# Turning x on VectorE in 32x32 squares through memory, and ScalarE's own SiLU for convolution and gate

## The chip, the cores and the metric

The kernel runs on one core of a Trainium2 chip. A core has TensorE (PE, matrix products, preceded by weight loads, PEld), VectorE (DVE), ScalarE (ACT), GpSimd (POOL) and SyncE (SP), which here only issues DMAs. Every engine works through its own list of instructions in order, and they meet only at semaphores. The metric is the device time of one execution in microseconds. The kernel before takes 1625.1 us, the median of three runs (1624.51 to 1627.74).

## The reference

The input is four sequences of 256 tokens with 512 channels. A small feed-forward layer (a base matrix and two of eight LoRA experts, picked for each token) stands before and after a Mamba2 mixer. Nearly all the time is in the mixer, cut here to what matters:

```python
proj = hidden_states @ in_proj_w.T                     # 512 -> 8192 (gate) + 10240 (x, B, C) + 128 (dt)
gate, xBC, dt = jnp.split(proj, [INTER, INTER + CONV_DIM], axis=-1)
conv = jax.lax.conv_general_dilated(xBC_t, conv_w, window_strides=(1,), padding=[(K - 1, 0)],
                                    feature_group_count=CONV_DIM)        # 4 taps, each channel by itself
xBC = jax.nn.silu(jnp.swapaxes(conv + conv_b[None, :, None], 1, 2))
x, Bm, Cm = jnp.split(xBC, [INTER, INTER + NG * SS], axis=-1)
# in chunks of 128 tokens, 128 heads of 64 channels in 8 groups:
Lmat = jnp.where(tri, jnp.exp(seg), 0.0)               # decay between two tokens
scores = jnp.einsum('bclhn,bcshn->bchls', Cc, Bc) * Lmat
Ydiag = jnp.einsum('bchls,bcshp->bclhp', scores, xdt)  # xdt = x * dt
y = Ydiag + Yoff + x * D
yg = y * jax.nn.silu(gate)
rstd = jax.lax.rsqrt(jnp.mean(jnp.square(yg_g), axis=-1, keepdims=True) + EPS)   # over a group of 1024
out = ((yg_g * rstd).reshape(Bsz, S, INTER) * norm_w) @ out_proj_w.T
```

silu(v) is v * sigmoid(v). Everything is float32.

## The kernel before

The projections are done in three passes of a rounded format (high times high, high times low, low times high), so each block of 128 input channels is three matmuls of 512 columns (L159 to L161). The two chunks of a sequence are treated as one block of 256 tokens with a causal mask, so no state is carried.

The mixer goes over 8 groups (index g) of 1024 channels and 16 heads. A group starts with four units (B and C, each for two halves of the tokens), which need the same projection, convolution and SiLU; then come 16 steps (index st). A step is one tile of 128 channels (two heads) for one half of the tokens, 512 columns. In a step, TensorE does the projection of x for the step four ahead (unit st+5, `project`), the projection of the gate (`project_gate`), the output projection of one tile of 128 tokens (`project_out`, in the first group only from step 8 on), and `mix_tokens`, which multiplies the 256x256 matrix of decays and scores with x. `mix_tokens` wants x with tokens on the partitions, whereas projection and convolution leave it with channels there. So a step begins with `transpose_x` (L1441): four 128x128 matmuls with the identity.

The other engines in a step, each in the order of its own list:

- ScalarE: four exponentials of 256 columns, the decay for the next step (`decay_from_first`, L1108, waits for the mask and for the `mix_tokens` that last used the slot); rounding of a weight tile (L834); in the steps from 9 on a copy of a finished output half (L1148); evacuation of the projection of x, times the last tap (L877); square of the gated y of the step before (L1140); rounding of a y tile for the output projection (L1131); four exponentials of 128 columns (`decay_from_second`, L1118); tanh for the gate (L1125); tanh for the convolution (L1097); in even steps the rounding of an output weight (L1088).
- VectorE: y plus D times x (`skip_y`, L1280), the product of decays and scores (`make_mix`, L1262), x times dt out of PSUM (`scale_x`, L1269), three taps of the convolution (L892), the rest of the SiLU for the gate (L1286) and for the convolution (L1244), in odd steps an output weight (L1290), in steps 1 to 8 two additions of the group before (L1309, L1316).
- GpSimd: the causal mask on the first diagonal (`mask_diagonals`, L1021, needs only its DMA) and on the second (L1025, waits for `mix_tokens`), both for the next step; y times gate (`gate_y`, L1033); the low part of a weight (L839); the low part of a y tile (`split_tile`, L1038); the running sum of squares (`sum_squares`, L1046, from step 3 on).
- SyncE: a weight tile (256 KB), the decay rows (512 KB, waits for L1118) and in odd steps an output weight (256 KB).

The group ends with a tail: the rest of the projections of the next group's B, C and first x, and the mean square, for which ScalarE loads the table of Sqrt (`root`, L1152) and then that of Exp again.

SiLU is computed as v/2 * (1 + tanh(v/2)); the halves are put into the taps, D and dt beforehand (`conv_constants`, `head_constants`). Tanh and Exp are in one table, so the steps load none.

Of the kernel before, what the change touches and what calls it, by code (L numbers as in the profile page):

```python
# [790 lines left out]
class InProj:  # L791
# [3 lines left out]
    def __init__(self, nc, ctx, m, w_in, conv_w, conv_b, d_skip):  # L795
        def sb(name, shape, dt=F32):
# [103 lines left out]
def mixer_phase(nc, m, ip, norm_w, w_out, ncs_dram, next_ln):  # L900

    with ExitStack() as ctx:
# [65 lines left out]
        def _(sp):  # L968
# [110 lines left out]
        def _(act):  # L1079
            start_at_one(act, [s["th"], s["tg"], s["decay"], s["sq"], s["wohi"], s["gcopy"], s["root"]])  # L1080
# [527 lines left out]
```

## Time and profile before

| | |
|---|---|
| median of 3 runs | 1625.1 us |
| profiled execution, its span | 1627.01 us, 1625.2 us |
| PE busy | 1564.3 us, 96% |
| PE weight loads busy | 1226.0 us, 75% |
| DVE busy | 1228.0 us, 76% |
| POOL busy | 1052.0 us, 65% |
| ACT busy | 1002.3 us, 62% |
| mean granted TensorE clock | 0.989 |
| DMA | 131.65 MB, mean 81 GB/s |

The span is what the trace covers; 1.8 us of the execution lie around it. Matmuls are pipelined: a matmul of 512 columns has a record of some 0.39 us, but the next one starts 0.23 us after it, so the sum of a group's records is more than the time it holds the engine. ScalarE's and VectorE's records overlap a little too, by about 0.1 us, and what an instruction costs in a row of others is the distance between two starts.

### The profile page before, as it was taken

The numbers are of one execution on the slowest core, as the hardware profiler recorded it, in microseconds if no ns is written. First come the engines' busy times: TensorE is split into PE (matmuls) and PEld (weight loads), VectorE is DVE, ScalarE is ACT, GpSimd is POOL, SyncE is SP. The second block draws the span as 40 slices with busy tenths as digits, with TensorE's granted clock in tenths as the row PEclk, the third lists the DMA queues.
The fourth block names the chain that finished last, engine by engine and source line by source line (L and its number), as shares of the span: only waits on it lengthen the run. The fifth ranks groups of instructions, "written<-read, shape, count | busy, mean of one in ns | idle before, by whom it ended". The sixth has DMA issues, their size and how long they took to land. (4 is left out here: it accounts for less than half of the span.)

```text
span 1625.2 us, 25474 instructions
## 1 busy us (share of the span) xinstructions
PE 1564.3 (96%) x8296; PEld 1226.0 (75%) x8296; DVE 1228.0 (76%) x1689; ACT 1002.3 (62%) x2122; POOL 1052.0 (65%) x790
## 2 busy tenths in 40 slices
PE   6979999999999999999999999999999999999979
PEld 4657777777777777777777777777777777777757
DVE  6688877787778877887688877887688877887565
ACT  4357765666666665666666665666666665666431
POOL 2017874788757874788657874787657874787620
PEclk9899999999999999999999999999999999999989
DMA  3033321323222221222212321223222221322011
GB/s 118 1 103 103 107 91 59 92 91 92 78 72 92 92 92 59 91 92 92 78 72 92 92 91 59 92 92 92 78 75 88 92 92 59 98 86 84 20 40 53
DMA packets 73658, 131.65 MB, mean 81 GB/s; under 512 B 10944, under 2 KB 10944, under 8 KB 73280
## 3 DMA queue, kind: packets, MB, share of 16 engines
q1 hardware_dynamic: 73536, 130.09, 24.3%
q8 instruction: 68, 1.11, 0.3%
q14 instruction: 54, 0.44, 0.1%
HBM read 127.44 MB, written 2.62 MB: 80 GB/s over the span
## 5 line engine op out<-in xcount | busy, mean ns | idle before, releaser
L892 DVE SCALAR_TENSOR_TENSOR mx_acc<-bank,mx_cw,mx_acc 128x510 f32<-128x510 f32 (+2 forms) x480 | 358.3, 746 | 160.8 <-ACT mx_acc L877 149.5
L159 PE MATMUL bank<-h_hi,mx_w_hi 128*128 128x512 f32 x1152 | 465.6, 404 | 4.4 <-DVE mx_acc L892 2.3
L161 PE MATMUL bank<-h_hi,mx_w_lo 128*128 128x512 f32 x1152 | 453.1, 393 | 0.0
L160 PE MATMUL bank<-h_lo,mx_w_hi 128*128 128x512 f32 x1152 | 450.2, 391 | 0.0
L1108 ACT ACTIVATE mx_mix<-mx_csb,mx_gncs 128x256 f32<-128x256 f32 x512 | 218.9, 499 | 284.3 <-PE bank L1478 281.3
L1033 POOL TENSOR_TENSOR mx_y<-mx_y,mx_sg 128x512 f32<-128x512 f32 x128 | 338.4, 2644 | 59.7 <-DVE mx_y L1280 51.7
L839 POOL TENSOR_TENSOR mx_w_lo<-mx_w_raw,mx_w_hi 128x512 fp32r<-128x512 f32 x144 | 187.4, 1302 | 111.0 <-ACT mx_w_hi L834 111.0
L161 PEld LDWEIGHTS bank<-h_hi,mx_w_lo 128*128 128x128 f32 x1152 | 216.9, 188 | 48.5
L159 PEld LDWEIGHTS bank<-h_hi,mx_w_hi 128*128 128x128 f32 x1152 | 217.3, 189 | 47.8 <-issue 6.5
L160 PEld LDWEIGHTS bank<-h_lo,mx_w_hi 128*128 128x128 f32 x1152 | 217.7, 189 | 41.5
L1262 DVE TENSOR_TENSOR mx_mix<-mx_mix,mx_cbt 128x1536 f32<-128x1536 f32 x128 | 224.5, 1754 | 0.0
L1025 POOL TENSOR_SCALAR_AFFINE_SELECT mx_mix<-mx_csb 128x512 f32<-128x512 f32 x128 | 89.9, 702 | 202.0 <-PE bank L1478 202.0
L877 ACT ACTIVATE mx_acc<-bank,mx_cb,mx_cw 128x512 f32<-128x512 f32 x160 | 124.2, 777 | 140.9 <-PE bank L161 140.9
L159 PE MATMUL bank<-mx_wo_hi,mx_yt_hi 128*128 128x512 f32 x512 | 203.4, 397 | 7.3 <-POOL mx_yt_lo L1038 7.3
L1038 POOL TENSOR_TENSOR mx_yt_lo<-mx_y,mx_yt_hi 128x512 fp32r<-128x512 f32 x128 | 167.3, 1307 | 58.2 <-ACT mx_yt_hi L1131 58.0
L161 PE MATMUL bank<-mx_wo_hi,mx_yt_lo 128*128 128x512 f32 x512 | 202.0, 394 | 0.0
L160 PE MATMUL bank<-mx_wo_lo,mx_yt_hi 128*128 128x512 f32 x512 | 200.5, 392 | 0.0
L1021 POOL TENSOR_SCALAR_AFFINE_SELECT mx_csb<-mx_csb 128x512 f32<-128x512 f32 x128 | 123.2, 963 | 68.1 <-DMA mx_csb<-cs_rows 68.1
L1280 DVE SCALAR_TENSOR_TENSOR mx_y<-mx_acc,mx_dh,bank 128x512 f32<-128x512 f32 x128 | 95.3, 745 | 88.9 <-PE bank L1478 88.8
L1118 ACT ACTIVATE mx_mix<-mx_mix,mx_gncs 128x128 f32<-128x128 f32 x512 | 162.1, 389 | 0.0
L1474 PE MATMUL bank<-mx_mix,mx_xd 128*64 128x256 f32 x1024 | 160.5, 392 | 0.0
L1046 POOL TENSOR_TENSOR mx_ssum<-mx_ssum,mx_sq 128x512 f32<-128x512 f32 x112 | 148.2, 1323 | 1.1 <-ACT mx_sq L1140 1.1
(163 smaller groups left out, 2203.7 us busy)
## 6 DMA issues: line engine op xcount, KB each, us to landing
mx_csb<-cs_rows SPq DMA_DIRECT2D x128, 512.0 KB, 4.0
mx_w_raw<-in_w_in SPq DMA_DIRECT2D x144, 256.0 KB, 4.0
mx_wo_raw<-in_w_out SPq DMA_DIRECT2D x64, 256.0 KB, 4.2
res<-in_x SPq DMA_DIRECT2D x8, 256.0 KB, 5.0
f_base_raw<-in_base_wt SPq DMA_DIRECT2D x2, 1024.0 KB, 6.1
out<-res SPq DMA_DIRECT2D x8, 256.0 KB, 2.0
f_a_raw<-in_lora_a SPq DMA_DIRECT2D x2, 256.0 KB, 3.8
f_lb_raw<-in_lora_b SPq DMA_DIRECT2D x2, 256.0 KB, 6.2
```

The lines of the kernel that those rows point to most:

```text
L159: nc.tensor.matmul(out, w_hi, x_hi, start=first, stop=False)
L160: nc.tensor.matmul(out, w_hi, x_lo, start=False, stop=False)
L161: return nc.tensor.matmul(out, w_lo, x_hi, start=False, stop=last)
L839: self.nc.gpsimd.tensor_tensor(self.w_lo[:, w % 3, :, :], self.w_raw[:, w % 3, :, :], self.w_hi[:, w % 3, :, :].bitcast(F32), ALU.subtract ...
L892: self.nc.vector.scalar_tensor_tensor(dst, src[:, :, 0:SEQ - k], self.cw[:, c, TAPS - 1 - k:TAPS - k], dst, ALU.mult, ALU.add).then_inc(s[ ...
L1033: nc.gpsimd.tensor_tensor(y[:, st, :], y[:, st, :], sg[:, st % 2, :], ALU.mult).then_inc(s["yg"], 1)
L1038: nc.gpsimd.tensor_tensor(yt_lo[:, p % 2, :, :], y_tile(q, hf, t), yt_hi[:, p % 2, :, :].bitcast(F32), ALU.subtract).then_inc(s["ylo"], 1)
L1046: nc.gpsimd.tensor_tensor(ssum[:, i, :], ssum[:, i, :], sq[:, i, :], ALU.add).then_inc(s["ssum"], 1)
L1108: nc.scalar.activation(mix[:, i, hd, b, 0:SEQ], csb[:, i, hd, b * SEQ:(b + 1) * SEQ], ACT.Exp, bias=gncs[:, tile, head:head + 1], scale=-1.0)
L1118: last = nc.scalar.activation(mix[:, i, hd, b, SEQ:PAIR], mix[:, i, hd, b, SEQ:PAIR], ACT.Exp, bias=gncs[:, tile, head:head + 1], scale=-1.0)
L1262: nc.vector.tensor_tensor(a, a, both, ALU.mult).then_inc(s["mix"], 1)
L1474: nc.tensor.matmul(Y_BANK[i][rows, c0:c0 + SEQ], xd[:, i, 2 * b, hd, :], mix[:, i, hd, b, 0:SEQ], start=True, stop=False)
```

## The change

**x is no longer transposed on TensorE.** VectorE transposes each 32x32 square of the tile in place (`turn_squares`), writing x with the squares laid out by partition block. SyncE writes that tile, 256 KB, to a buffer in memory and reads it back with four DMAs, one for each block of 32 partitions, so that the squares come to lie in their transposed places (`move_x`). `scale_x` reads the result from SBUF instead of PSUM and stands behind the taps now, not in front of them.

**SiLU is one instruction on ScalarE** (`silu_conv`, `silu_gate`), in place for the convolution. The two VectorE instructions that finished it are gone, and so are the factors 0.5.

**ScalarE's list has another order.** The rounding of the y tile and the square of the step before stand at the end of the step, behind the SiLUs; before, they stood ahead of the second exponentials. The squares are written into the gate's buffer, which is free by then. The exponentials take their bias straight from the whole table `ncs`.

```diff
+            def move_x(g, st):
+                i, u = st % 2, st + 4
+                sp.wait_ge(s["turned"], 1 + STEPS * g + st + 1)
+                if not (first(g) and st < 2):
+                    x_moved(sp, *((g, st - 2) if st >= 2 else (g - 1, st + STEPS - 2)))
+                sp.dma_start(x_dram[i, :, :], xs[:, u % 2, :]).then_inc(x_out[i], 16)
+                step_slot_freed(sp, s["xd"], g, st)
+                sp.wait_ge(x_out[i], 16 * (XT * g + st // 2 + 1))
+                for q in range(P // SQ):
+                    src = x_dram[i, :, q * P:(q + 1) * P].rearrange("(i r) e -> r i e", r=SQ)
+                    sp.dma_start(xt[q * SQ:(q + 1) * SQ, i, :, :, :].rearrange("r i t c -> r i (t c)"),
+                                 src).then_inc(x_in[i], 16)
...
-            def tanh_conv(g, u):
+            def silu_conv(g, u):
                 act.wait_ge(s["tap"], 1 + (TAPS - 1) * (UNITS * g + u + 1))
-                act.wait_ge(s["conv"], 1 + UNITS * g + max(u - 1, 0))
-                nc.scalar.activation(th[:, u % 2, :], acc[:, u % 4, :, :].rearrange("p b t -> p (b t)"),
-                                     ACT.Tanh).then_inc(s["th"], 1)
+                a = acc[:, u % 4, :, :].rearrange("p b t -> p (b t)")
+                nc.scalar.activation(a, a, ACT.Silu).then_inc(s["conv"], 1)
...
-                nc.scalar.activation(sg[:, st % 2, :], G_BANK[:, :], ACT.Tanh, scale=0.5).then_inc(s["tg"], 1)
+                nc.scalar.activation(sg[:, st % 2, :], G_BANK[:, :], ACT.Silu).then_inc(s["sg"], 1)
...
+                    if here or more:
+                        decay_from_second(gn, stn)
+                    silu_gate(g, st)
+                    if here or more:
+                        silu_conv(gn, un)
+                    if st % 2 == 0:
+                        split_wo(g, st // 2)
+                    if here and has_tile(g, st + 1):
+                        round_tile(g, st + 1)
                     if st >= 1:
                         square(g, st - 1)
...
-                    if here and has_tile(g, st + 1):
-                        round_tile(g, st + 1)
...
+            def turn_squares(g, st):
+
+                u = st + 4
+                dve.wait_ge(s["conv"], 1 + UNITS * g + u + 1)
+                if not (first(g) and st < 2):
+                    x_moved(dve, *((g, st - 2) if st >= 2 else (g - 1, st + STEPS - 2)))
+                nc.vector.transpose(xs[:, u % 2, :].rearrange("p (q t c) -> p t q c", t=2 * HB, c=SQ),
+                                    acc[:, u % 4, :, :].rearrange("p b t -> p (b t)")).then_inc(s["turned"], 1)
...
                     make_mix(g, st)
-                    scale_x(g, st)
...
                         ip.taps(dve, gn, un)
-                    silu_gate(g, st)
-                    if here or more:
-                        silu_conv(gn, un)
+                    scale_x(g, st)
+                    if here:
+                        turn_squares(g, st + 1)
...
-                    transpose_x(g, st)
```

**ScalarE's list, a step from 9 on, before.** From the evacuation of the projection to the first exponentials of the next step. `mx_th` is the tanh of the convolution, `mx_sg` the gate, `mx_sq` the square, `mx_yt_hi` the rounded y tile; the brackets name the semaphores that an instruction waits for.

```order
L877 ACTIVATE mx_acc<-bank,mx_cb,mx_cw 128x512 [waits mx_ysb,mx_proj]
L1140 ACTIVATE mx_sq<-mx_y 128x512 [waits mx_ssum,mx_yg]
L1131 ACTIVATE mx_yt_hi<-mx_y 128x512 [waits mx_out,mx_yg]
L1118 ACTIVATE mx_mix<-mx_mix,mx_gncs 128x128 [waits mx_masked1]
L1118 ACTIVATE mx_mix<-mx_mix,mx_gncs 128x128 x3
L1125 ACTIVATE mx_sg<-bank 128x512 [waits mx_yg,mx_gate]
L1097 ACTIVATE mx_th<-mx_acc 128x512 [waits mx_conv,mx_tap]
L1108 ACTIVATE mx_mix<-mx_csb,mx_gncs 128x256 [waits mx_y,mx_masked0]
```

The same stretch now. L1143 and L1111 are the SiLUs of gate and convolution, L1149 rounds the y tile, L1156 is the square.

```order
L879 ACTIVATE mx_acc<-bank,mx_cb,mx_cw 128x512 [waits mx_ysb,mx_proj]
L1131 ACTIVATE mx_mix<-mx_mix,ncs 128x128 [waits mx_masked1]
L1131 ACTIVATE mx_mix<-mx_mix,ncs 128x128 x3
L1143 ACT_TABLE_LOAD [waits mx_ssum]
L1143 ACTIVATE mx_sg<-bank 128x512 [waits mx_gate]
L1111 ACTIVATE mx_acc<-mx_acc 128x512 [waits mx_tap]
L1149 ACTIVATE mx_yt_hi<-mx_y 128x512 [waits mx_out,mx_yg]
L1156 ACTIVATE mx_sg<-mx_y 128x512 [waits mx_yg]
L1121 ACT_TABLE_LOAD [waits mx_y]
L1121 ACTIVATE mx_mix<-mx_csb,ncs 128x256 [waits mx_masked0]
```

Two table loads stand in every step now, one before the SiLUs and one before the exponentials; the whole program had 22 and has 273. Square and y tile have moved from the middle to the end.

**GpSimd's list** keeps its order (only the buffer of the squares has another name). This is it now, around the border of two steps; it reads what ScalarE's moved instructions leave.

```order
L1052 TENSOR_TENSOR mx_yt_lo<-mx_y,mx_yt_hi 128x512 [waits mx_yhi]
L1060 TENSOR_TENSOR mx_ssum<-mx_ssum,mx_sg 128x512 [waits mx_ssum,mx_sq]
L1035 AFFINE_SELECT mx_csb<-mx_csb 128x4x128 [waits mx_cs_in1]
L1039 AFFINE_SELECT mx_mix<-mx_csb 128x4x128 [waits mx_y]
L1047 TENSOR_TENSOR mx_y<-mx_y,mx_sg 128x512 [waits mx_sg,mx_ysb]
```

L1035 is the first mask, for which ScalarE's L1121 waits (`mx_masked0`); it stands behind the sum of squares, as before.

**VectorE's list, an odd step from 9 on, before**, from `make_mix` to the next `make_mix`:

```order
L1262 TENSOR_TENSOR mx_mix<-mx_mix,mx_cbt 128x1536 [waits mx_decay]
L1269 TENSOR_TENSOR mx_xd<-bank,mx_gdt 128x512 [waits mx_y,mx_xt]
L892 SCALAR_TENSOR_TENSOR mx_acc<-bank,mx_cw,mx_acc 128x2x255 [waits mx_evac]
L892 SCALAR_TENSOR_TENSOR mx_acc<-bank,mx_cw,mx_acc 128x2x254 [waits mx_tap]
L892 SCALAR_TENSOR_TENSOR mx_acc<-bank,mx_cw,mx_acc 128x2x253 [waits mx_tap]
L1286 SCALAR_TENSOR_TENSOR mx_sg<-mx_sg,bank 128x512 [waits mx_tg]
L1244 SCALAR_TENSOR_TENSOR mx_acc<-mx_th,mx_acc 128x512 [waits mx_th]
L1290 SCALAR_TENSOR_TENSOR mx_wo_lo<-mx_wo_raw,mx_nw,mx_wo_hi 128x512 [waits mx_wohi]
L1280 SCALAR_TENSOR_TENSOR mx_y<-mx_acc,mx_dh,bank 128x512 [waits mx_ylo,mx_y]
L1262 TENSOR_TENSOR mx_mix<-mx_mix,mx_cbt 128x1536 [waits mx_decay]
```

and now:

```order
L1272 TENSOR_TENSOR mx_mix<-mx_mix,mx_cbt 128x1536 [waits mx_decay]
L894 SCALAR_TENSOR_TENSOR mx_acc<-bank,mx_cw,mx_acc 128x2x255 [waits mx_evac]
L894 SCALAR_TENSOR_TENSOR mx_acc<-bank,mx_cw,mx_acc 128x2x254 [waits mx_tap]
L894 SCALAR_TENSOR_TENSOR mx_acc<-bank,mx_cw,mx_acc 128x2x253 [waits mx_tap]
L1288 TENSOR_TENSOR mx_xd<-mx_xt,mx_gdt 128x4x4x32 [waits mx_y,mx_x_in1]
L1280 STREAM_TRANSPOSE mx_xs<-mx_acc 128x4x4x32 [waits mx_x_in0,mx_conv]
L1304 SCALAR_TENSOR_TENSOR mx_wo_lo<-mx_wo_raw,mx_nw,mx_wo_hi 128x512 [waits mx_wohi]
L1299 SCALAR_TENSOR_TENSOR mx_y<-mx_acc,mx_dh,bank 128x512 [waits mx_ylo,mx_y]
L1272 TENSOR_TENSOR mx_mix<-mx_mix,mx_cbt 128x1536 [waits mx_decay]
```

The scaling of x (L1288) stands behind the taps, and the turning of the next x (L1280) behind it, waiting for ScalarE's SiLU.

## Rows read from the trace of the kernel before

**Rows 1.** Windows: two steps of group 0, one whole group (each column: busy us, instructions).

```profile
145.95:162.28 16.33, 15.18 (x88) 11.63 (x88) 13.96 (x18) 12.13 (x27) 13.39 (x10) 1.00 0.35 113
465.06:647.25 182.19, 180.39 (x978) 142.29 (x977) 141.39 (x180) 117.94 (x253) 129.74 (x96) 1.00 0.26 85
```

**Rows 2.** Timeline of PE at a step's border (start, duration, line).

```profile
715.64 0.66 PE L1447 MATMUL bank<-ident,mx_acc 128*128 128x128 f32 x4
716.06 0.48 PE L159 MATMUL bank<-h_hi,mx_w_hi 128*128 128x512 f32 x1
```

**Rows 3.** Timeline of ACT, a whole even step from 9 on (brackets: idle before, releaser).

```profile
564.50 1.71 ACT L1108 ACTIVATE mx_mix<-mx_csb,mx_gncs 128x256 f32<-128x256 f32 x4 [3.01 <-PE bank L1478]
566.11 0.62 ACT L834 ACTIVATE mx_w_hi<-mx_w_raw 128x512 fp32r<-128x512 f32 x1
566.64 0.58 ACT L1148 ACTIVATE gacc<-bank 128x512 f32<-128x512 f32 x1
567.79 0.78 ACT L877 ACTIVATE mx_acc<-bank,mx_cb,mx_cw 128x512 f32<-128x512 f32 x1 [0.58 <-PE bank L161]
568.47 0.62 ACT L1140 ACTIVATE mx_sq<-mx_y 128x512 f32<-128x512 f32 x1
568.99 0.62 ACT L1131 ACTIVATE mx_yt_hi<-mx_y 128x512 fp32r<-128x512 f32 x1
569.51 1.26 ACT L1118 ACTIVATE mx_mix<-mx_mix,mx_gncs 128x128 f32<-128x128 f32 x4
570.68 0.58 ACT L1125 ACTIVATE mx_sg<-bank 128x512 f32<-128x512 f32 x1
571.16 0.62 ACT L1097 ACTIVATE mx_th<-mx_acc 128x512 f32<-128x512 f32 x1
571.68 0.71 ACT L1088 ACTIVATE mx_wo_hi<-mx_wo_raw,mx_nw 128x512 fp32r<-128x512 f32 x1
574.79 1.71 ACT L1108 ACTIVATE mx_mix<-mx_csb,mx_gncs 128x256 f32<-128x256 f32 x4 [2.39 <-PE bank L1478]
```

**Rows 4.** Timeline of ACT around a table load in a tail.

```profile
279.41 0.63 ACT L1097 ACTIVATE mx_th<-mx_acc 128x512 f32<-128x512 f32 x1 [2.00 <-DVE mx_acc L892]
280.06 1.28 ACT L1152 ACT_TABLE_LOAD   x1
281.35 0.21 ACT L1152 ACTIVATE mx_rms<-mx_rms 128x8 f32<-128x8 f32 x1
```

**Rows 5.** Timeline of POOL in the step of rows 3.

```profile
569.69 1.30 POOL L1038 TENSOR_TENSOR mx_yt_lo<-mx_y,mx_yt_hi 128x512 fp32r<-128x512 f32 x1 [0.42 <-ACT mx_yt_hi L1131]
570.95 1.30 POOL L1046 TENSOR_TENSOR mx_ssum<-mx_ssum,mx_sq 128x512 f32<-128x512 f32 x1
572.20 1.09 POOL L1021 TENSOR_SCALAR_AFFINE_SELECT mx_csb<-mx_csb 128x512 f32<-128x512 f32 x1
575.56 2.74 POOL L1033 TENSOR_TENSOR mx_y<-mx_y,mx_sg 128x512 f32<-128x512 f32 x1
```

**Rows 6.** Timeline of DVE in the same stretch.

```profile
571.90 0.90 DVE L1244 SCALAR_TENSOR_TENSOR mx_acc<-mx_th,mx_acc 128x512 f32<-128x512 f32 x1
575.39 1.75 DVE L1262 TENSOR_TENSOR mx_mix<-mx_mix,mx_cbt 128x1536 f32<-128x1536 f32 x1
578.89 2.31 DVE L892 SCALAR_TENSOR_TENSOR mx_acc<-bank,mx_cw,mx_acc 128x510 f32<-128x510 f32 x3 [1.15 <-ACT mx_acc L877]
```

**Rows 7.** Single lines: duration in ns, least/median/most, of all their instructions.

```profile
L1021 POOL TENSOR_SCALAR_AFFINE_SELECT mx_csb<-mx_csb x128: 624/1087/1105, 102.5 to 1514.0; 128x512 f32<-128x512 f32 x128
L1033 POOL TENSOR_TENSOR mx_y<-mx_y,mx_sg x128: 1261/2734/2792, 122.6 to 1535.2; 128x512 f32<-128x512 f32 x128
L1244 DVE SCALAR_TENSOR_TENSOR mx_acc<-mx_th,mx_acc x160: 679/891/1605, 101.0 to 1524.0; 128x512 f32<-128x512 f32 x160
L1316 DVE SCALAR_TENSOR_TENSOR res<-gacc,mx_rms,res x64: 744/752/1760, 299.2 to 1575.7; 128x512 f32<-128x512 f32 x64
```

**Rows 8.** DMA issues: KB each, median us from issue to landing.

```profile
mx_csb<-cs_rows SPq DMA_DIRECT2D x128, 512.0 KB, 4.0
```

More of the change, by code:

```diff
@@ L53 @@
 PAIR = SEQ + CH
+SQ = 32
+CONSTS = 7
 NE, RANK = 8, 16
@@ L800, in __init__ @@
         self.s = semaphores(nc, ctx, "mx", [
-            "const_in", "nw_in", "const", "proj", "gate", "xt", "y", "cb", "out", "ss",
-            "evac", "th", "tg", "decay", "sq", "yhi", "whi", "wohi", "gcopy", "root",
+            "const_in", "nw_in", "const", "proj", "gate", "turned", "y", "cb", "out", "ss",
+            "evac", "decay", "sq", "yhi", "whi", "wohi", "gcopy", "root",
             "tap", "conv", "mix", "xd", "sg", "ysb", "cbt", "gsum", "outsb", "ms", "inv", "wolo",
@@ L907, in mixer_phase @@
         wo_in = [ctx.enter_context(nc.semaphore(f"mx_wo_in{i}")) for i in range(2)]
+        x_out, x_in = ([ctx.enter_context(nc.semaphore(f"mx_x_{n}{i}")) for i in range(2)] for n in ("out", "in"))
         cs_in = [ctx.enter_context(nc.semaphore(f"mx_cs_in{i}")) for i in range(2)]
@@ L1005, in group @@
                         ip.load_constants(sp, g + 1)
+                    move_x(g, st)
                 if more:
                     load_late(g + 1)
-            loop_groups(sp, group)
+            for g in range(NG):
+                group(g, g + 1 < NG)
         @block.gpsimd
@@ L1079, in _ @@
         def _(act):
[L1080 removed]
+            start_at_one(act, [s["conv"], s["sg"], s["decay"], s["sq"], s["wohi"], s["gcopy"], s["root"]])
             start_after_quad(act, [s["yhi"]])
@@ L1116, in decay_from_second, with silu_gate @@
                     for hd in range(2):
-                        tile, head = 2 * (HB * hf + b) + 1, 2 * j + hd
+                        tile, head = 2 * (HB * hf + b) + 1, GH * g + 2 * j + hd
                         last = nc.scalar.activation(mix[:, i, hd, b, SEQ:PAIR], mix[:, i, hd, b, SEQ:PAIR], ACT.Exp,
-                                                    bias=gncs[:, tile, head:head + 1], scale=-1.0)
+                                                    bias=m.ncs[:, tile, head:head + 1], scale=-1.0)
                 last.then_inc(s["decay"], 1)
-            def tanh_gate(g, st):
+            def silu_gate(g, st):
                 act.wait_ge(s["gate"], 1 + STEPS * g + st + 1)
-                act.wait_ge(s["yg"], 1 + STEPS * g + max(st - 1, 0))
-                nc.scalar.activation(sg[:, st % 2, :], G_BANK[:, :], ACT.Tanh, scale=0.5).then_inc(s["tg"], 1)
+                if st >= 4:
+                    act.wait_ge(s["ssum"], 1 + SUMS * g + st - 3)
+                elif st >= 2:
+                    act.wait_ge(s["yg"], 1 + STEPS * g + st - 1)
+                elif not first(g):
+                    act.wait_ge(s["ssum"], 1 + SUMS * g - 1 + st)
+                nc.scalar.activation(sg[:, st % 2, :], G_BANK[:, :], ACT.Silu).then_inc(s["sg"], 1)
             def round_tile(g, p):
@@ L1232, in _ @@
         def _(dve):
-            start_at_one(dve, [s["conv"], s["mix"], s["xd"], s["sg"], s["ysb"], s["cbt"],
+            start_at_one(dve, [s["turned"], s["mix"], s["xd"], s["ysb"], s["cbt"],
                                s["ms"], s["inv"], s["wolo"]])
@@ L1422, in _ @@
         def _(pe):
-            start_at_one(pe, [s["gate"], s["xt"], s["y"], s["cb"], s["ss"]])
+            start_at_one(pe, [s["gate"], s["y"], s["cb"], s["ss"]])
             start_after_quad(pe, [s["out"]])
@@ L1439, in b_dot_c @@
                 last.then_inc(s["cb"], 1)
-            def transpose_x(g, st):
-                pe.wait_ge(s["conv"], 1 + UNITS * g + st + 5)
-                if st == 0:
-                    pe.wait_ge(s["ms"], 1 + g)
-                pe.wait_ge(s["xd"], 1 + STEPS * g + st)
-                for t in range(2 * HB):
-                    last = nc.tensor.transpose(T_BANK[:, t * P:(t + 1) * P],
-                                               acc[:, st % 4, t // 2, t % 2 * CH:(t % 2 + 1) * CH], m.ident[:, :])
-                last.then_inc(s["xt"], 1)
             def project_gate(g, st):
@@ L1555, in program @@
 def program(nc, x, w_in, w_dt, conv_w, conv_b, dt_bias, d_skip, norm_w, w_out, base_wt, router_wt, lora_a, lora_b,
-            ncs_dram, out):
+            ncs_dram, x_dram, out):
     m = Chip()
```

120 lines of the change are left out of this document (46 added, 74 removed).

## The prediction

> **What bounds the kernel now.** I read the windows first. A whole group takes 182.19 us and TensorE is busy in 180.39 of them at full granted clock, the other engines in 118 to 141 [rows 1]. TensorE sets the time, so 7 groups at 182.19 and a shorter first one make up nearly all of the span. The step is next, in ScalarE's timeline: from one first L1108 to the next 10.29 us pass (564.50 to 574.79), and before each it sits idle for 3.01 or 2.39 us until the matmuls of L1478 end [rows 3]. ScalarE is ready 2.4 to 3 us early. In group 0, steps without an output projection take 16.33 / 2 = 8.17 us [rows 1]. The third view is GpSimd in the same step: its mask for the next step, L1021, ends at 572.20 + 1.09 = 573.29, 1.5 us before the L1108 that needs it [rows 5, 3]. These two margins are what the change spends.
>
> **Part 1, the transposes go.** From the first transpose to the first projection 0.42 us pass (715.64 to 716.06) [rows 2]. TensorE's step shrinks from 10.29 to about 9.85 us, -0.42 x 128 = -54 us if nothing else comes to bound.
>
> **Part 2, two table loads a step.** A step's ScalarE work before, from the distances of starts [rows 3]: 1.61 (L1108), 0.53 (L834), 0.48 (L1148, 0.58 less the 0.1 that neighbours overlap), 0.68 (L877), 0.52 (L1140), 0.52 (L1131), 1.17 (L1118), 0.48 (L1125), 0.52 (L1097), 0.61 (L1088): 7.1 us, 6.5 in odd steps, 0.48 less in steps up to 8. A load takes 1.28 us, starts 0.02 us after the end of the instruction before (279.41 + 0.63 = 280.04 to 280.06), and the next starts 0.01 us after it [rows 4]; it also undoes one overlap of 0.1. So 1.41 us each. For the SiLU instructions I take tanh's durations; half to twice of them would be -0.5 to +1.1 us a step. ScalarE then has 8.8 to 9.9 us of work in a step, on average 9.4: by itself it would just fit under TensorE's 9.85.
>
> The Trainium skill, "ScalarE: Activation LUTs", section "What ACT_TABLE_LOAD costs", adds a drain of 1380 ns to the load's 1283 ns. The 0.02 us ahead of the load in rows 4 don't show it; with it the forecast below would be 1.38 x 124 = 171 us longer.
>
> **Part 3, the new order closes a loop through GpSimd.** L1021 for step st+2 stands on GpSimd behind the sum of squares of st-1, and that behind the low part of the y tile st+1. Both now wait for the last instructions of ScalarE's step, and the next step's exponentials wait for L1021. So a step from 3 on can't be shorter than: ScalarE from its exponentials to the end of the y tile, then GpSimd's three instructions. With t = 0 at the first exponential (odd step up to 8, no L1148, no L1088): L834 at 1.61, L877 at 2.13, second exponentials 2.81 to 4.08, load 4.10 to 5.38, gate 5.39, convolution 5.87 (its taps began at 2.95 and are done at 5.3, 2.31 us [rows 6]), y tile 6.39 to 7.01. GpSimd starts 0.08 us after the y tile's end (568.99 + 0.62 = 569.61 to 569.69) [rows 3, 5]: 7.09. Then 1.26 and 1.25 us, the distances of its starts, and 0.62 for L1021, its least [rows 5, 7]: 10.22, plus 0.07 to ScalarE's start: 10.29. Even steps have L1088 as well (+0.6), steps from 9 on L1148 (+0.48): 10.29, 10.89, 10.77, 11.37. The second load hides in this wait: the square ends at 7.5, the load at 8.8.
>
> **Part 4, what VectorE does meanwhile.** `gate_y` takes 1.26 us at least but 2.73 in the median [rows 7]: L1033 began at 575.56, 0.17 us into L1262, which ended at 577.14, and itself ended at 578.30, 1.16 us later [rows 5, 6]. It stood still for the whole of L1262. The other way round L1244, 0.68 alone, took 0.90 when it began at 571.90 during the sum of squares (to 572.25), and L1021 behind it 1.09 for 0.62 [rows 5 to 7]. All these VectorE instructions read two operands in SBUF. So one works while the other waits, in the order of asking.
>
> The Trainium skill, "SBUF — State Buffer", section "SBUF: two separate sides", calls this an exclusive lock between GpSimd and VectorE instructions with two SBUF inputs, held to the instruction's end. Rows 5 and 6 agree; by a shared bandwidth the sum would be that of the next rival.
>
> Before, L1262 met only `gate_y`, which nobody waited for. Now the three GpSimd instructions end the step, where VectorE has its output weight (odd, 0.75), the addition L1316 (steps 1 to 8, 0.75 [rows 7]) and L1262 (1.75). I take the turning as an instruction of one operand that holds nobody up, of 0.69 us like one of 512 columns; its bounds are 0.5 and twice that. In turn, in us from t = 0:
> - odd, to 8: y tile to 8.4; output weight asked 7.2, runs to 9.1; squares to 10.35; L1316 asked 9.8, runs to 11.07; mask to 11.6. Step 11.7.
> - even, to 8: y tile 7.7 to 9.0; L1316 to 9.7; squares to 10.95; L1262, asked at 10.35, to 12.65; mask to 13.2. Step 13.25.
> - odd, from 9: y tile to 8.9; output weight to 9.6; squares to 10.85; L1262 to 12.55; mask to 13.1. Step 13.15.
> - even, from 9: y tile 8.2 to 9.5; L1262 to 11.2; squares to 12.4; mask to 13.05. Step 13.1.
>
> **Part 5, the way through memory.** A turned tile leaves VectorE at t = 7.2 to 7.7 and is wanted by `scale_x` behind the taps, at 5.3 of the next step: 10 to 11 us of room. No row shows such a transfer. The nearest is the 512 KB load with 4.0 us from issue to landing [rows 8]; a write and a read at that make 8, and three more issues at some 0.4 us each 9.2 us as upper end, perhaps 4 at the lower. I take 7, hidden in the steps. At a group's start nothing covers it: `scale_x` of step 0 follows the last turn directly, and I charge 2 us a group (0 to 4). `scale_x` and `mix_tokens` end at about t = 8, before the mask, so neither the moved scaling nor TensorE's wait for it is late. SyncE waits for the write before it can issue the next decay rows; these are wanted a step later than they land. Four small copies of constants at a group's border are below 1 us.
>
> **The sum.** Steps 3 to 14 of a group: 3 x (11.7 + 13.25) + 3 x (13.15 + 13.1) = 153.6 against 12 x 10.29 = 123.5: +30.1. Steps 1 and 2 have no sum of squares in the chain and gain together 0.4. The start costs 2. In the last step TensorE ends at t = 7.8 and not at 10.3, and the tail follows it: -2.5. Together +29.2, x 7 = +204. Group 0: steps 7 and 8 +4.4, 9 to 14 +17, steps 3 to 6 (no y tile: 9.65 and 11.25, against 8.17) +9.1, start and steps 0 to 2 +6: +36.5. In all 1625.2 + 241 = 1866 us of span, 1868 of execution. The profiled execution is 1.9 us above the median, which I take off: **1866 us**.
>
> **The rivals.**
> - *The lock costs less.* If VectorE's operands delay the chain not at all, the steps are 10.29 to 11.37, on average 10.83, +5.4 a group after start and tail, group 0 +16: 1625 + 38 + 16 = 1679. Half of the lock gives about 1770. For it: the order of asking in part 4 is worked out, and an instruction that comes 0.3 us earlier slips in ahead. Against it: rows 5 and 6. 20% for the stretch between 1680 and 1790.
> - *Faster.* If the mask doesn't hang on the moved instructions as I read it, because GpSimd gets square and y tile early enough (it would need to get them 2 us earlier than in part 3), then TensorE's 9.85 us bound and ScalarE's 9.4 fit: 1625 - 54 + 16 (eight starts through memory) = 1587. It decides where the chain of part 3 falls under 9.85. For it: all engines have less than 9.9 us of work. Against: the chain without any lock is 10.29 at least. 8% for everything under 1622.
> - *The change does nothing measurable*, gain and loop in balance: 2%.
> - *Memory or the clock bounds.* If the way through memory takes over 11 us, each us more costs 1 us x 120 steps; or a load costs more than in rows 4; or TensorE, now idle for a quarter of a step, is granted less. 10% for more than 1900, some 1960.
>
> 60% are left for 1790 to 1900 with 1866 as its value. Range over all: 1700 to 1905. What a measurement of this kernel can tell is about 0.2%, 3 us: faster 0.08, same 0.02, slower 0.90.
>
> **What will show it.** In ScalarE's timeline the time before the first exponentials of a step is ended by GpSimd's mask, no longer by L1478's matmuls, some 2 to 4 us of it; the load before them costs nothing extra and lies in that wait, the load before the gate follows at once on the second exponentials. The step is 11.7 to 13.3 us long. L1021's counterpart has a median of 0.6 to 2.3 us. TensorE's waits in the steps are ended by the scaling of x, 2 to 3 us a step, and its busy share falls to 80 to 85%. 256 table loads of 1.28 us are in the steps' code. I am wrong if the exponentials wait for TensorE, if ScalarE has no idle time in a step, or if `scale_x` waits for its DMA in the middle of a group.

## The result: 1863.4 us, 14.6% slower, and the profile after

| | before | after |
|---|---|---|
| median of 4 runs each, us | 1626.07 (1624.51 to 1627.74) | 1863.36 (1862.45 to 1865.07) |
| ratio after to before, 95% interval | | 1.146 (1.144 to 1.148) |
| profiled execution: time and span, us | 1627.01, 1625.2 | 1862.45, 1860.6 |
| a whole group, us | 182.19 [rows 1] | 210.97 |

The head of the page of the changed kernel (busy us, share of the span, instructions):

```profile
span 1860.6 us, 24204 instructions
PE 1581.7 (85%) x7784; PEld 1215.5 (65%) x7784; DVE 1226.8 (66%) x1545; ACT 1321.1 (71%) x2373; POOL 1047.1 (56%) x790
```

A window over its first whole group, from one L1168 table load in a tail to the next. The columns, as in [rows 1]: start and end, length, then busy us (instructions) of PE, PEld, DVE, ACT and POOL, granted clock of TensorE, busy share of the DMA engines, GB/s.

```profile
316.99:527.96 210.97, 186.63 (x915) 143.65 (x913) 141.05 (x161) 157.38 (x285) 129.34 (x97) 0.94 0.35 113
```

TensorE was busy in 99% of a group and is now busy in 88%, with 63 fewer instructions. Its granted clock over the group is 0.94, where it was 1.00 [rows 1]. No engine is full: as the rows below show, the step is a ring of engines that wait for each other. Its waits (engine, line, what ended the wait: total us, times, longest):

```profile
POOL mx_yt_lo L1052 <- ACT mx_yt_hi L1149: 430.8, 118, 7.5
DVE mx_acc L894 <- ACT mx_acc L879: 421.2, 152, 6.5
ACT mx_mix L1121 <- POOL mx_csb L1035: 262.3, 106, 3.4
PE bank L1466 <- DVE mx_xd L1288: 235.4, 101, 6.5
```

Third row: ScalarE's first exponentials wait for GpSimd's mask 106 times. In [rows 3] TensorE ended that wait. One step (even, below 9), first ScalarE (compare [rows 3]), then GpSimd [rows 5], then VectorE [rows 6]. Here and below `...` stands for rows left out, and a row of exponentials with x2 or x1 in place of x4 is cut off by the end of the view:

```profile
572.63 1.71 ACT L1121 ACTIVATE mx_mix<-mx_csb,ncs 128x256 f32<-128x256 f32 x4 [1.86 <-POOL mx_csb L1035]
...
575.43 1.27 ACT L1131 ACTIVATE mx_mix<-mx_mix,ncs 128x128 f32<-128x128 f32 x4
576.71 1.28 ACT L1143 ACT_TABLE_LOAD   x1
578.01 0.60 ACT L1143 ACTIVATE mx_sg<-bank 128x512 f32<-128x512 f32 x1
578.50 0.62 ACT L1111 ACTIVATE mx_acc<-mx_acc 128x512 f32<-128x512 f32 x1
...
579.63 0.62 ACT L1149 ACTIVATE mx_yt_hi<-mx_y 128x512 fp32r<-128x512 f32 x1
580.15 0.62 ACT L1156 ACTIVATE mx_sg<-mx_y 128x512 f32<-128x512 f32 x1
580.79 1.28 ACT L1121 ACT_TABLE_LOAD   x1
585.48 0.91 ACT L1121 ACTIVATE mx_mix<-mx_csb,ncs 128x256 f32<-128x256 f32 x2 [3.40 <-POOL mx_csb L1035]
```

```profile
580.33 1.31 POOL L1052 TENSOR_TENSOR mx_yt_lo<-mx_y,mx_yt_hi 128x512 fp32r<-128x512 f32 x1 [3.12 <-ACT mx_yt_hi L1149]
581.59 1.74 POOL L1060 TENSOR_TENSOR mx_ssum<-mx_ssum,mx_sg 128x512 f32<-128x512 f32 x1
583.29 2.16 POOL L1035 TENSOR_SCALAR_AFFINE_SELECT mx_csb<-mx_csb 128x512 f32<-128x512 f32 x1
```

```profile
580.55 1.64 DVE L1330 SCALAR_TENSOR_TENSOR res<-gacc,mx_rms,res 128x512 f32<-128x512 f32 x1
...
582.77 2.18 DVE L1272 TENSOR_TENSOR mx_mix<-mx_mix,mx_cbt 128x1536 f32<-128x1536 f32 x1
```

Follow the ring: exponentials 572.63, load, gate, convolution, y tile to 580.25; GpSimd's low half from 580.33; the sum; the mask, which asks at 583.29 while VectorE's L1272 runs to 584.95, and ends at 585.45; exponentials at 585.48. The step is 12.85 us. In the same rows VectorE and GpSimd take turns, and the one that begins while the other runs lasts longer: L1330 (0.75 alone) ends 0.55 us after L1052, L1060 1.14 us after L1330, L1272 1.62 us after L1060, L1035 0.50 us after L1272.

### The profile page after: what moved, and what is told of

Its sections match the earlier page's. It is cut to its first block and busy times, and to the rows that moved or that the text cites. A ratio compares the mean times of both kernels' runs of the same rounds, so it can differ in the third digit from the quotient of the medians.

```text
span 1860.6 us, 24204 instructions
## 1 busy us (share of the span) xinstructions
PE 1581.7 (85%) x7784; PEld 1215.5 (65%) x7784; DVE 1226.8 (66%) x1545; ACT 1321.1 (71%) x2373; POOL 1047.1 (56%) x790
## 5 line engine op out<-in xcount | busy, mean ns | idle before, releaser
L161 PE MATMUL bank<-h_hi,mx_w_hi 128*128 128x512 f32 x1152 | 485.6, 422 | 4.9 <-DVE mx_acc L894 3.0
L162 PE MATMUL bank<-h_lo,mx_w_hi 128*128 128x512 f32 x1152 | 462.6, 402 | 0.0
L1052 POOL TENSOR_TENSOR mx_yt_lo<-mx_y,mx_yt_hi 128x512 fp32r<-128x512 f32 x128 | 167.0, 1305 | 430.8 <-ACT mx_yt_hi L1149 430.8
L1121 ACT ACTIVATE mx_mix<-mx_csb,ncs 128x256 f32<-128x256 f32 x512 | 219.0, 499 | 262.7 <-POOL mx_csb L1035 262.3
L1466 PE MATMUL bank<-mx_mix,mx_xd 128*64 128x256 f32 x1024 | 181.3, 436 | 235.8 <-DVE mx_xd L1288 235.4
L1272 DVE TENSOR_TENSOR mx_mix<-mx_mix,mx_cbt 128x1536 f32<-128x1536 f32 x128 | 277.4, 2167 | 0.0
L1466 PEld LDWEIGHTS bank<-mx_mix,mx_xd 128*64 128x64 f32 x1024 | 63.6, 148 | 288.4 <-DVE mx_xd L1288 287.0
L1047 POOL TENSOR_TENSOR mx_y<-mx_y,mx_sg 128x512 f32<-128x512 f32 x128 | 225.1, 1759 | 15.7 <-DVE mx_y L1299 15.5
L1035 POOL TENSOR_SCALAR_AFFINE_SELECT mx_csb<-mx_csb 128x512 f32<-128x512 f32 x128 | 191.1, 1493 | 68.4 <-DMA mx_csb<-cs_rows 68.4
L1060 POOL TENSOR_TENSOR mx_ssum<-mx_ssum,mx_sg 128x512 f32<-128x512 f32 x112 | 202.0, 1804 | 42.4 <-ACT mx_sg L1156 42.4
L1131 ACT ACTIVATE mx_mix<-mx_mix,ncs 128x128 f32<-128x128 f32 x512 | 162.3, 391 | 0.0
```

Source lines behind the costliest of these rows:

```text
L161: nc.tensor.matmul(out, w_hi, x_hi, start=first, stop=False)
L162: nc.tensor.matmul(out, w_hi, x_lo, start=False, stop=False)
L1035: nc.gpsimd.affine_select(out=rows[:, :, 0:CH], in_=rows[:, :, 0:CH], compare_op=ALU.is_ge, fill=MASKED, base=0, pattern=[[0, 2 * HB], [1, ...
L1047: nc.gpsimd.tensor_tensor(y[:, st, :], y[:, st, :], sg[:, st % 2, :], ALU.mult).then_inc(s["yg"], 1)
L1052: nc.gpsimd.tensor_tensor(yt_lo[:, p % 2, :, :], y_tile(q, hf, t), yt_hi[:, p % 2, :, :].bitcast(F32), ALU.subtract).then_inc(s["ylo"], 1)
L1060: nc.gpsimd.tensor_tensor(ssum[:, i, :], ssum[:, i, :], sg[:, i, :], ALU.add).then_inc(s["ssum"], 1)
```

## The experiments

Twelve kernels, each timed in at least 4 runs beside the kernel before. Medians in us, ratios to before with 95% intervals:

| kernel | starts from | median | ratio |
|---|---|---|---|
| e5 new order on ScalarE alone | before | 1769.98 | 1.090 (1.087 to 1.092) |
| e11 e5, mask first | before | 1625.65 | 1.000 (0.999 to 1.001) |
| e7 ScalarE's SiLU alone | before | 1643.60 | 1.011 (1.009 to 1.013) |
| e6 x through memory alone | before | 1654.17 | 1.018 (1.015 to 1.021) |
| e62 e6, mask first | before | 1639.66 | 1.008 (1.005 to 1.011) |
| e2 mask first | after | 1603.72 | 0.987 (0.985 to 0.988) |
| e8 e2 without step loads | after | 1601.08 | 0.984 (0.981 to 0.986) |
| e1 order of before | after | 1653.30 | 1.018 (1.016 to 1.020) |
| e9 e1, mask first | after | 1667.24 | 1.027 (1.024 to 1.030) |
| e10 e1, make_mix early | after | 1635.51 | 1.006 (1.004 to 1.008) |
| e3 make_mix early | after | 1755.68 | 1.081 (1.079 to 1.083) |
| e4 tanh, no step loads | after | 1782.41 | 1.097 (1.095 to 1.099) |

### Open the loop at the mask (e2): right, and faster than before

```
 GpSimd, step st:  low half of w_in
+                  first mask of step st+2      (moved up)
                   low half of the y tile
                   sum of squares
-                  first mask of step st+2
```

> The changed kernel with one move on GpSimd alone: the first mask for step st+2 stands ahead of the y tile and of the sum of squares instead of behind them. ScalarE's list is untouched. Theory: nothing that ScalarE's exponentials need hangs on the end of its own step any more, so 1620 us as in the run with the old order (1600 to 1650); the exponentials' idle time is no longer ended by the mask. Rivals (loads; memory): 1863, since neither changes.

Measured: 1603.72 us, 260 less than the change by the place of one GpSimd instruction. ScalarE's timeline of a whole step (first mask L1035, exponentials L1131 here):

```profile
666.78 1.71 ACT L1131 ACTIVATE mx_mix<-mx_csb,ncs 128x256 f32<-128x256 f32 x4
...
675.36 1.28 ACT L1131 ACT_TABLE_LOAD   x1 [0.43 <-PE bank L1480]
676.65 1.71 ACT L1131 ACTIVATE mx_mix<-mx_csb,ncs 128x256 f32<-128x256 f32 x4
```

The wait over the whole kernel (no exponentials wait for the mask in this run):

```profile
ACT L1131 <- PE bank L1480: 64.9, 91, 1.7
```

The step is 9.87 us, and TensorE again ends ScalarE's wait. So within the steps of a whole group everything in the change but the mask's place behind the y tile fits under TensorE, as parts 1 to 3 of the prediction had it for an open loop. This is the fastest version here that computes SiLU, 1.3% under before.

### Put ScalarE's order back (e1): the loop goes, a second wait comes

```
 ScalarE, step st: exponentials, w_hi, evacuation,
+                  square, y tile               (moved up)
                   second exponentials, gate, convolution, wo_hi
-                  y tile, square
```

> The changed kernel with ScalarE's square and y tile back ahead of the second exponentials; loads, SiLU and the way through memory stay. Theory (loop through GpSimd): GpSimd gets the y tile at t = 4 instead of 7 to 8 us, its mask is done before ScalarE has finished its own 8.9 to 10 us, and the step falls from 11.1 to 12.9 us to that or to TensorE's 9.85: 1620 us (1600 to 1645). Rival (the two loads a step are themselves what costs, 2 x 1.41 us or more in ScalarE's list): the loads are all still there, the step stays above 11 us, over 1800. Rival (way through memory): no change, 1863.

Measured: 1653.30 us, 210 less than the change, but over the range. No exponentials wait for the mask any more. Steps below 9 now alternate between 9.83 and 11.72 us. A step of 11.71 us (724.55 to 736.26), ScalarE, GpSimd and VectorE:

```profile
729.59 0.63 ACT L1156 ACTIVATE mx_sg<-mx_y 128x512 f32<-128x512 f32 x1 [2.13 <-POOL mx_y L1047]
726.82 2.74 POOL L1047 TENSOR_TENSOR mx_y<-mx_y,mx_sg 128x512 f32<-128x512 f32 x1 [2.91 <-DVE mx_y L1299]
726.65 1.75 DVE L1272 TENSOR_TENSOR mx_mix<-mx_mix,mx_cbt 128x1536 f32<-128x1536 f32 x1
```

The same wait over the whole kernel, among ScalarE's waits:

```profile
ACT mx_sg L1156 <- POOL mx_y L1047: 75.7, 61, 3.5
```

The square, now early, waits 61 times for `gate_y` (L1047), and that takes 2.74 us because `make_mix` (L1272) began 0.17 us before it. I had priced `gate_y` as work nobody waits for, as it was in before.

### Is it the mask or gate_y (e9, e10)?

e9 has the edits of e1 and e2. e10 has that of e1 and this one on VectorE:

```
+                  if st == 0: make_mix(g, 0)
-                  make_mix(g, st)
                   taps; scale_x(g, st)
+                  make_mix(g, st + 1)
                   turn_squares(g, st + 1)
```

> The changed kernel with both edits, ScalarE's order of before (e1_order_back_b) and the mask first (e2_mask_first_b). Theory (what is left in e1 is not the mask but ScalarE's square, which stands first in that order and waits for GpSimd's gate_y): as e1, 1650 us, range 1635 to 1660. Rival (e1 still has a wait through the mask): 1600 to 1610, as e2.

> The changed kernel with ScalarE's order of before (e1_order_back_b) and make_mix of the next step moved behind scale_x (e3_mix_early_b). Theory (in e1 GpSimd's gate_y takes 2.7 us because it runs beside make_mix, and ScalarE's square waits for it; with make_mix elsewhere gate_y is back at 1.3): e1's steps of 11.72 us go to 10 to 10.3, 1620 us, range 1600 to 1640. Rival (the steps of 11.72 us are ScalarE's list with its two loads, whatever gate_y does): 1653, as e1.

Measured: e9 1667.24 us, e10 1635.51. With e1's order the mask's place is worth nothing (e9 is even 14 us above e1, 7 over my range; why, is open). The other way round, e9 and e2 differ in ScalarE's order alone: once the mask stands first, the change's new order takes 1604 us and the old one 1667. The order that closed the loop is worth 64 us when the loop is open (with tanh and the transposes, e11 against before, it is worth nothing). Moving `make_mix` wins 18 us. GpSimd's `gate_y` in e1 (by line: busy us, mean ns), then in e10:

```profile
L1047 POOL TENSOR_TENSOR mx_y<-mx_y,mx_sg 128x512 f32<-128x512 f32 x128 | 338.9, 2648 | 215.0 <-DVE mx_y L1299 213.7
```

```profile
L1047 POOL TENSOR_TENSOR mx_y<-mx_y,mx_sg 128x512 f32<-128x512 f32 x128 | 165.5, 1293 | 180.2 <-DVE mx_y L1299 179.6
```

What the square waits for it in e10:

```profile
ACT mx_sg L1156 <- POOL mx_y L1047: 36.8, 26, 3.8
```

2648 ns became 1293 and the square's wait halved, from 75.7 to 36.8 us. What remains isn't explained by `gate_y`'s length: it also starts late, as its own waits for `skip_y` (L1299) are 179.6 us in e10. So the cause named in both expectations is there, but in e10 it gave 18 us of the 33 forecast (1635.51 is inside the range of 1600 to 1640): the steps of 11.72 us didn't go to 10 to 10.3, steps 4 to 8 of a group still alternate, between 9.2 to 10.1 and 10.6 to 11.3 us.

### Take the lock off the mask alone (e3)

The VectorE edit of e10, on the changed kernel with its own ScalarE order.

> The changed kernel with VectorE's 1536-element product for step st+1 moved ahead of the turning, away from GpSimd's last three instructions. Theory (one works in SBUF while the other waits): steps of 12.0, 11.6, 11.45 and 11.4 us (odd and even up to 8, odd and even from 9) for 11.1, 12.9, 12.7 and 12.9: 10 us a group less, 1785 us (1750 to 1815), and GpSimd's square sum and mask no longer stretched to over 2 us. Rival (the lock is a small part, VectorE is simply late): within 10 us of 1863, or slower, as the scaling of x is as late as before and the turning 1.7 us later.

Measured: 1755.68 us, 108 less than the change and inside the range. Steps 3 to 13 are 11.33 to 11.48 us. GpSimd's first mask by line (busy us, mean ns), in the change and then in e3:

```profile
L1035 POOL TENSOR_SCALAR_AFFINE_SELECT mx_csb<-mx_csb 128x512 f32<-128x512 f32 x128 | 191.1, 1493 | 68.4 <-DMA mx_csb<-cs_rows 68.4
```

```profile
L1035 POOL TENSOR_SCALAR_AFFINE_SELECT mx_csb<-mx_csb 128x512 f32<-128x512 f32 x128 | 98.2, 767 | 68.7 <-DMA mx_csb<-cs_rows 68.7
```

What the exponentials wait for it in e3, for 262.3 us in the change:

```profile
ACT mx_mix L1121 <- POOL mx_csb L1035: 175.6, 101, 2.6
```

So `make_mix` at this place is worth 108 us of the loss, and the mask itself is 93 us shorter. The loop remains without it.

### Take the loads out (e4, e8)

`ACT.Silu` becomes `ACT.Tanh` twice, so that a step loads no table; what comes out is the tanh, not the SiLU. e8 does it on top of e2.

> The changed kernel with the function Tanh in the place of Silu in both instructions, so that the steps load no table (the result is then not SiLU). The order stays the new one. Theory: the load ahead of the gate is 1.41 us inside the loop, the other is hidden; without it the three GpSimd instructions end at t = 8.9 to 10, before VectorE's product, which hangs on mix_tokens at t = 7.8, comes in their way, so the lock's part shrinks too: 1650 us (1620 to 1690). Simple reading (only the load's own 1.41 us x 124): 1688. If each load costs a drain of 1.38 us on top, 2 x 2.66 us a step less where ScalarE bounds: far below 1620.

> As e2_mask_first_b (the changed kernel with GpSimd's mask ahead of its y tile and sum), but with tanh for SiLU on ScalarE, so that no step loads a table; its output is not the reference's. Theory (with the loop through the mask open the loads lie in ScalarE's waits for TensorE, 64.9 us of which are left in e2): 1598 us, range 1588 to 1606. Rival (the 32 loads of a group cost what they cost anywhere): at least 40 of the 330 us of loads come off, under 1564.

Measured: e4 1782.41 us, only 81 less than the change, and a clear miss (1620 to 1690 were expected). ScalarE and GpSimd of e4, an odd step from 9 on:

```profile
604.16 1.71 ACT L1121 ACTIVATE mx_mix<-mx_csb,ncs 128x256 f32<-128x256 f32 x4 [4.70 <-POOL mx_csb L1035]
...
609.92 0.63 ACT L1111 ACTIVATE mx_acc<-mx_acc 128x512 f32<-128x512 f32 x1 [0.73 <-DVE mx_acc L894]
610.46 0.61 ACT L1149 ACTIVATE mx_yt_hi<-mx_y 128x512 fp32r<-128x512 f32 x1
...
616.29 0.91 ACT L1121 ACTIVATE mx_mix<-mx_csb,ncs 128x256 f32<-128x256 f32 x2 [4.71 <-POOL mx_csb L1035]
```

```profile
614.11 2.15 POOL L1035 TENSOR_SCALAR_AFFINE_SELECT mx_csb<-mx_csb 128x512 f32<-128x512 f32 x1
```

Without the load the convolution arrives before its taps are done and waits 0.73 us. The load had stood in that gap, so the y tile comes 6.30 us into the step, for 6.87 in the change, and the step shrinks by as much (12.70 to 12.13). The mask still runs into `make_mix` (2.15), which I had expected it to escape. e8 took 1601.08 us, inside its range, against 1603.72 in e2: in an open loop 251 loads of 1.28 us, 321 us of ScalarE, are worth 2.6 us (the ratios differ by 0.3%), which the intervals of the two ratios don't separate from nothing.

### Each part alone, on the kernel before (e5, e11, e7, e6, e62)

e5: the reverse of e1's diff on the kernel before. e11: e2's diff on top of e5.

> The kernel before with one edit: ScalarE issues the square and the y tile of a step behind the second exponentials, the gate's and the convolution's function and wo_hi, as the changed kernel does. Tanh on ScalarE, VectorE's two products for SiLU and TensorE's transposes stay; no table is loaded within a step. Theory (the order alone closes the loop ScalarE's y tile -> GpSimd's y tile, sum and mask -> exponentials): the convolution's tanh waits for the taps (6.4 us into the step), the y tile stands at 7.1 to 7.8, the mask ends near 12.2, so steps of about 12.2 us in place of 10.3 from step 3 on, + 7 x 12 x 1.9 = 160 at the most: 1760 us, range 1700 to 1800. Rival (order and table loads only cost together, since without the loads the y tile comes 2.6 us earlier): 1625 to 1650.

> As e5_new_order_alone (the kernel before with the new order on ScalarE, which took 1770 us), and GpSimd's mask ahead of its y tile and sum. Theory (all of the 145 us of e5 is the loop through the mask): back to TensorE's steps of 10.3 us, 1628 us, range 1615 to 1645. Rival (the y tile behind the taps is late for something else too, TensorE's w_out products or the sum): over 1660.

Measured: 1769.98 and 1625.65 us, both inside their ranges. The new order alone costs 145 us, without any table load or transfer of x. Putting the mask first takes all of it back (ratio to before 1.0002, 0.9992 to 1.0012). With e4 the whole loss adds up: 145 us for the order (before to e5), 12 for the rest without loads (e5 to e4), 81 for the loads (e4 to the change). ScalarE and GpSimd of e5, at the end of a step of 12.10 us that began at 601.63:

```profile
613.73 1.71 ACT L1108 ACTIVATE mx_mix<-mx_csb,mx_gncs 128x256 f32<-128x256 f32 x4 [4.68 <-POOL mx_csb L1021]
```

```profile
611.54 2.16 POOL L1021 TENSOR_SCALAR_AFFINE_SELECT mx_csb<-mx_csb 128x512 f32<-128x512 f32 x1
```

e7 has before's order and transposes, `ACT.Silu` in place of `ACT.Tanh`, and no products for SiLU on VectorE. e6 has x through memory, with tanh, VectorE's products and before's ScalarE order. e62 adds e2's diff to e6.

> The kernel before with ScalarE's own SiLU for convolution and gate, two table loads of 1.28 us in each step and VectorE's two products gone; ScalarE's order and TensorE's transposes are those of before. Theory (the loads make ScalarE's own list as long as the step: 7.2 and 7.9 us of list in odd and even steps plus 2.6 is 9.8 and 10.5 against 10.3): a small loss, 1640 us, range 1625 to 1665; the order and not the loads carries most of the 237 us. Rival (two loads in a step cost their full 2 x 1.28 us whatever the order): 1625 + 7 x 16 x 2.56 = 1910 us.

> The kernel before with the way of x through memory alone: squares turned on VectorE, written and read back by DMA, no transposes on TensorE; tanh on ScalarE and VectorE's two products for SiLU stay, and ScalarE's order is that of before. Theory (the way through memory is hidden and the end of each step is TensorE's): 0.42 us less in each of 96 steps of seven and a half groups is -40, the start of each group gives back up to 2 us of it: 1595 us, range 1585 to 1612. Rival (VectorE, which now turns squares as well and keeps its products, or the DMA behind it, is late with scale_x): 1625 or more.

> As e6_x_through_memory, and besides GpSimd masks the tile of the step after next ahead of the y tile's low half and the sum (the edit of e2_mask_first_b). Theory: steps are TensorE's 9.85 us with or without it, so the same as e6 within 5 us, about 1592 us (1580 to 1608), and below e2_mask_first_b's 1604 by the table loads that still stood in the way of group starts and tails. Rival (GpSimd's mask still holds some steps of e6): e62 over 10 us faster than e6.

Measured: e7 1643.60 us. Within a group its steps stay at 10.29 us (685.31 to 695.59), since the second load lies where ScalarE waits for TensorE. The first two steps of a group lose 3.2 us (8.9 and 11.4 for 6.7 and 10.5), of which the tail gives back 1.4; group 0 ends 5.4 us later. A step from the middle of a group:

```profile
685.31 1.71 ACT L1107 ACTIVATE mx_mix<-mx_csb,mx_gncs 128x256 f32<-128x256 f32 x4
...
694.30 1.28 ACT L1107 ACT_TABLE_LOAD   x1 [1.45 <-PE bank L1454]
695.59 1.71 ACT L1107 ACTIVATE mx_mix<-mx_csb,mx_gncs 128x256 f32<-128x256 f32 x4
```

e6 took 1654.17 us and missed (1585 to 1612), as its rival had it, by which VectorE, with the turning and its two products, is late. Steps 4 to 9 of a group alternate between 10.4 and 11.3 us; from 10 on most are at TensorE's 9.87. VectorE's rows in a step of 11.32 us, with the wait of the gate's product, L1269, for ScalarE:

```profile
542.21 0.69 DVE L1269 SCALAR_TENSOR_TENSOR mx_sg<-mx_sg,bank 128x512 f32<-128x512 f32 x1 [1.08 <-ACT mx_sg L1147]
542.82 1.27 DVE L1264 SCALAR_TENSOR_TENSOR mx_acc<-mx_xs,mx_acc 128x512 f32<-128x512 f32 x1
```

ScalarE in turn has its square waiting for `gate_y`, and its first exponentials for the mask:

```profile
ACT mx_sg L1160 <- POOL mx_y L1048: 145.0, 82, 4.6
ACT mx_mix L1125 <- POOL mx_csb L1036: 99.2, 62, 2.1
```

e62 is 14.5 us under e6 (I expected 5 at most) and still above before: its rival, that the mask holds some steps of e6, was right. So the way through memory doesn't pay alone, even with the mask first (+15 us); alone the two parts cost 29 and 19 us, together with the new order and an open loop they win 21. e62 differs from e2 both in the SiLU, which empties VectorE, and in ScalarE's order. Which of them it lacks isn't shown by a run of its own, but e9, with the SiLU and the order of before, loses 42 us, so the SiLU by itself isn't enough.

## Why the prediction was right, step by step

**Part 1** (TensorE's step 9.85 us): 9.87 in e2.

**Part 2** (a load 1.28 us, at once behind its predecessor, gate and convolution at tanh's durations): 576.71 stands 0.01 us after the end of L1131, the two take 0.60 and 0.62. No drain of 1380 ns is to be seen. The sum named in the prediction from the Trainium skill, "ScalarE: Activation LUTs", section "What ACT_TABLE_LOAD costs", would have come out 171 us longer, at 2037.

**Part 3** (the loop): shown. e5 makes it alone, e2 and e11 open it. For the even step it had the y tile's low half start at t = 7.7: it started at 580.33 - 572.63 = 7.70.

**Part 4** (taking turns): the order of asking was right at each place in the even step. Each handover is 0.05 to 0.15 us cheaper than reckoned, 0.4 together: L1330 ends at 582.19, 0.55 after L1052's end and not 0.7, L1060 1.14 after that and not 1.25, L1272 at 584.95, 1.62 after L1060's and not 1.70, the mask 0.50 after that and not 0.55. Steps were forecast at 11.7, 13.25, 13.15, 13.1 us and measured at 11.15, 12.86, 12.71, 12.86. Eleven of the steps 3 to 14 are together 4.6 us shorter than forecast. The twelfth, 14, is 14.20 us for 13.1, and I had missed why:

```profile
498.94 1.28 ACT L1121 ACT_TABLE_LOAD   x1 [4.27 <-POOL mx_csb L1035]
500.24 1.71 ACT L1121 ACTIVATE mx_mix<-mx_csb,ncs 128x256 f32<-128x256 f32 x4
```

Here the load itself waits for the mask and stands on the path with all its 1.28 us. In the other steps it runs ahead and the exponentials behind it wait.

**Part 5** (7 us through memory, hidden): write and reads take 2.0 us each from issue to landing, where I had taken the 4.0 of [rows 8], and a read is issued every 0.43 us. The DMA issues (KB each, median us from issue to landing):

```profile
x_squares<-mx_xs SPq DMA_DIRECT2D x128, 256.0 KB, 2.0
mx_xt<-x_squares SPq DMA_DIRECT2D x512, 64.0 KB, 2.0
```

By line (busy us, mean ns, idle time before and what ended it), `scale_x`:

```profile
L1288 DVE TENSOR_TENSOR mx_xd<-mx_xt,mx_gdt 128x512 f32<-128x512 f32 x128 | 88.4, 691 | 2.0 <-DMA mx_xt<-x_squares 2.0
```

So over the whole kernel `scale_x` waits 2.0 us for its transfer. With 2.0 + 2.0 + 3 x 0.43 plus the issues it is nearer 6 us than 7.

**The sum** per group: steps 3 to 14 +26.6 (forecast +30.1), steps 1 and 2 -1.2 (-0.4), start +4.5 (+2), tail -0.8 (-2.5), together 29.1 against 29.2. Group 0 ends 36.9 us later (+36.5). The start is the term that was mis-sized most. I charged it the transfer alone, which isn't waited for there: `scale_x` doesn't follow the last turn directly, as I had it, but stands behind the taps, which end at 536.02, and starts at 535.93. What ends step 0 is the mask, as in the other steps:

```profile
541.91 0.51 ACT L1121 ACTIVATE mx_mix<-mx_csb,ncs 128x256 f32<-128x256 f32 x1 [2.02 <-POOL mx_csb L1035]
```

That 1866 came within 3 us of 1863 owes something to luck. These errors cancel: -3.5, -0.8, +2.5, +1.7. The spans are 5.4 us apart (1866 forecast, 1860.6 measured), since I multiplied 29.2 by 7 and the last group, with none behind it, ends only 23.4 us longer. Half of that is hidden by the 1.9 us that I took off because the profiled execution had been above the median; this one is 0.9 below it. The mechanism and its place owe nothing to luck.

**The signs** named beforehand are there: the mask ends the exponentials' wait (262.3 us in 106 waits, 2.5 us each), its median is 1.10 us (0.6 to 2.3 was named), TensorE waits 2.3 us a time for the scaled x and is busy for 85% of the span.

**The rivals.** "Faster, 1587" was named with its condition, that the mask doesn't hang on the moved instructions. e2 makes that condition true and takes 1604. Of the 17 us between, 10.5 lie in group 0: its table load in the tail, L1178, stands at 285.86, where that of before stood at 280.06, so it loses 5.8 us where the sum (-54 over eight groups, 2 for the start) had it gain 4.7. The cause is open, and so is that of the rest (at group starts TensorE waits up to 6.5 us for the scaled x). "The lock costs less" falls by the steps, 12.86 us where it had 10.89, and by e3, 108 us for one of the lock's places.

## What to carry to other kernels

When an instruction is moved later on one engine, follow who waits for it through the next engine's queue, since an unrelated instruction queued behind the waiting one (here a mask for the step after next) may be what ends the step. Look for a place ahead of the wait before giving up the change: one instruction moved up turned +14.6% into -1.3%. And judge a costly instruction by the gap it stands in: a pair of table loads, 2.56 us, was worth next to nothing in a wait and 0.6 us in a step of the loop, and one load its full 1.28 where it waited itself.

## What the runs showed of the hardware that was not expected

- VectorE's turning of 32x32 squares isn't part of the taking of turns with GpSimd. In e10 it ran its usual 0.71 us inside the sum of squares (GpSimd's row first, then VectorE's), and the sum ended 1.16 us after `make_mix` did (723.39), less than its 1.25 alone [rows 5]. Over the 128 of the changed kernel the turning takes 0.70 to 0.72 us:

```profile
721.73 2.82 POOL L1060 TENSOR_TENSOR mx_ssum<-mx_ssum,mx_sg 128x512 f32<-128x512 f32 x1
721.20 2.19 DVE L1272 TENSOR_TENSOR mx_mix<-mx_mix,mx_cbt 128x1536 f32<-128x1536 f32 x1 [0.58 <-ACT mx_mix L1131]
723.63 0.71 DVE L1280 STREAM_TRANSPOSE mx_xs<-mx_acc 128x512 f32<-128x512 f32 x1 [0.24 <-ACT mx_acc L1111]
```

- Exponentials and SiLU need a table load at each switch, both ways; squares, copies with a scale, and conversions between them need none (the rows of the even step above: load before L1143, load before L1121, none between L1143 and the square).
- A table load may take over the wait of the instruction behind it, as in step 14.
- TensorE idle for an eighth of a group was granted 0.94 of its full clock there, for 1.00 before. In the steps the mask and not TensorE ends ScalarE's wait, so I don't count the clock as a cause; no run tests it by itself. e2, whose TensorE is busy for 95% of the span, has 0.981 over all.
